# Layer norm stage of an attention and mixture-of-experts kernel written out two tiles ahead, with its row sums on two other engines and the expert padding moved to the setup

## The reference, cut to what matters

```python
x = x + gnn(layernorm(x), adj, W_q, b_q, W_k, b_k, W_v, b_v)
x = x + ffn(layernorm(x), Wr, Wg_s, Wu_s, Wd_s, Wg, Wu, Wd)

# gnn
q = e @ W_q.T + b_q;  k = e @ W_k.T + b_k;  v = e @ W_v.T + b_v
z = (q @ k.T) / sqrt(512) * adj
z = where(z == 0, -10000, z)
out = relu(softmax(z, axis=1) @ v)

# ffn: router softmax over 8 experts, the top 2 of each row with a softmax of their weights
shared = (silu(X @ Wg_s) * (X @ Wu_s)) @ Wd_s
out = shared + sum over the chosen experts of weight * (silu(X @ Wg[e]) * (X @ Wu[e])) @ Wd[e]
```

## Time and profile before

| what | us |
|---|---|
| median of three runs | 1493.55 |
| the profiled execution | 1493.32 |
| its span (first to last instruction) | 1491.6 |
| TensorE busy | 1425.8 (96%) |
| VectorE busy | 681.7 (46%) |
| ScalarE busy | 438.0 (29%) |
| GpSimd busy | 175.4 (12%) |

### The profile page before, as it was taken

One profiled execution on the slowest core, in us unless ns is written; L12 is line 12 of the kernel. 1 busy time (PEld: TensorE's weight loads), 2 busy tenths in 40 slices (PEclk: granted clock), 3 DMA queues, 4 the chain that ended last, 5 costly groups with the idle time before them and its releaser, 6 DMA issues.

```text
span 1491.6 us, 20252 instructions
## 1 busy us (share of the span) xinstructions
PE 1425.8 (96%) x7140; PEld 1227.6 (82%) x7140; DVE 681.7 (46%) x1465; ACT 438.0 (29%) x683; POOL 175.4 (12%) x233
## 2 busy tenths in 40 slices
PE   5889999999999998489999999999999999999998
PEld 3768888888888876369898989889898989888887
DVE  4875566566566565424234332424233435232222
ACT  2331221221221234124334332424233434231111
POOL 1220012112112122001101011010101010100000
PEclk8999999999999999789999999999999999999999
DMA  7311123223223156517252525134252525441000
GB/s 272 123 64 71 57 71 113 70 70 113 70 70 112 67 174 212 56 46 210 50 191 36 191 43 187 35 84 141 43 191 43 184 60 173 111 151 57 0 29 29
DMA packets 85888, 151.75 MB, mean 102 GB/s; under 512 B 14512, under 2 KB 24752, under 8 KB 83504
## 3 DMA queue, kind: packets, MB, share of 16 engines
q1 hardware_dynamic: 68672, 117.79, 24.1%
q0 software_dynamic: 9760, 18.93, 6.5%
q10 hardware_dynamic: 7392, 14.16, 2.8%
HBM read 109.90 MB, written 42.01 MB: 102 GB/s over the span
## 4 chain that ended last, share of the span: by engine, by line
PE 92%; issue 3%; DVE 2%; ACTq 1%; DMA 1%; ACT 0%; POOL 0%; DVEq 0%; SPq 0%; POOLq 0%
PE bank L230 86%; PE bank L649 2%; ACTq L925 1%; PE bank L671 1%; PE bank L802 1%; PE bank L851 1%; DMA owners<-owner,idx 0%; PE bank L665 0%; PE bank L599 0%; PE bank L579 0%; PE bank L809 0%; DMA wq_raw<-in_L_gnn_W_q_dram 0%; PE bank L621 0%; DVE stat L1153 0%; ACT v_h L892 0%
## 5 line engine op out<-in xcount | busy, mean ns | idle before, releaser
L1481 DVE TENSOR_TENSOR hid<-bank,hid 128x384 f32<-128x384 f32 (+1 forms) x96 | 57.8, 602 | 364.6 <-PE bank L230 364.6
L230 PE MATMUL bank<-dn_h,hT_h 128*128 128x512 f32 x416 | 168.3, 405 | 0.9 <-DVE counts L1380 0.6
L230 PE MATMUL bank<-dn_h,hT_l 128*128 128x512 f32 x416 | 163.9, 394 | 0.0
L230 PE MATMUL bank<-dn_l,hT_h 128*128 128x512 f32 x416 | 163.6, 393 | 0.0
L230 PE MATMUL bank<-xq_h,gate_h 128*128 128x384 f32 (+1 forms) x384 | 137.0, 357 | 4.7 <-DVE gate_l L1149 4.4
L230 PE MATMUL bank<-xq_h,gate_l 128*128 128x384 f32 (+1 forms) x384 | 136.6, 356 | 0.0
L230 PE MATMUL bank<-xq_l,gate_h 128*128 128x384 f32 (+1 forms) x384 | 136.5, 355 | 0.0
L230 PE MATMUL bank<-xq_h,up_h 128*128 128x384 f32 (+1 forms) x384 | 135.5, 353 | 0.0
L230 PE MATMUL bank<-xq_h,up_l 128*128 128x384 f32 (+1 forms) x384 | 135.4, 353 | 0.0
L230 PE MATMUL bank<-xq_l,up_h 128*128 128x384 f32 (+1 forms) x384 | 135.3, 352 | 0.0
L1050 ACT ACTIVATE hid<-bank 128x384 f32<-128x384 f32 (+1 forms) x96 | 50.6, 527 | 233.0 <-PE bank L230 232.9
(11 more groups left out here) (213 smaller groups left out, 2751.0 us busy)
## 6 DMA issues: line engine op xcount, KB each, us to landing
adj_t<-in_adj_dram SPq DMA_DIRECT2D x16, 1024.0 KB, 5.8
gate_raw<-in_L_ffn_Wg_dram SPq DMA_DIRECT2D x16, 1024.0 KB, 5.6
up_raw<-in_L_ffn_Wu_dram SPq DMA_DIRECT2D x16, 1024.0 KB, 10.2
dn_raw<-in_L_ffn_Wd_dram SPq DMA_DIRECT2D x16, 1024.0 KB, 12.4
x_t<-in_x_dram SPq DMA_DIRECT2D x32, 256.0 KB, 6.4
slots<-x2row ACTq DMA_DIRECT2D x8, 1024.0 KB, 11.8
e_x<-slots ACTq DMA_DIRECT2D x22, 256.0 KB, 2.7
acc<-x SPq DMA_DIRECT2D x16, 256.0 KB, 2.0
```

What stands on the lines that cost most here:

```text
L230: mm = pe.matmul(o, lhs(a, c), rhs(b, c), start=first and n == 1, stop=last and n == 3 * len(chunks))
L1481: dve.tensor_tensor(hid[:, c % 2, 0:w], bank[2 + c % 2][:, 0:w], hid[:, c % 2, 0:w], ALU.mult).then_inc(sem("hid"), 1)
```

## The change

1. The weights of q and k are loaded, copied and subtracted in four parts each, with a semaphore for each part. The first c2 matmul waits for one part instead of the whole. The first two tiles of x are loaded ahead of W_v.
2. The bias products come directly after c2, in bank 7. The order on TensorE is now: c2, biases, A chunks 0 and 1, turning W_v, A chunk 2, turn tile 0, A chunk 3, turn tile 1.
3. `before_attention` is gone. Each engine runs 16 tiles without a loop, turned and normalised two tiles ahead of the values. ScalarE writes xnT_h directly and VectorE xnT_l directly; xT_h, xT_l and GpSimd's copy are gone. x has four places in place of two.
4. The row sum is made by GpSimd (xn times c2 into "spent") and ScalarE (a copy that sums, directly into s_q).
5. The two halves of the first queries stand ahead of the values of tiles 14 and 15.
6. ScalarE issues the clearing in 12 transfers of 512 KB (32 rows of each of the eight regions, from 32 partitions), one in each of the first 12 tiles, for 384 rows a region instead of 512. `owners` is filled whole in the setup by one transfer of 80 partitions.
7. The rows e_x are loaded as soon as the scatters have landed; the padding comes after, writes `slots` only, and never begins inside the first 384 slots. The table takes two more small VectorE operations.
8. The pieces of block 0 are spread by a plan over all eight chunks.

```diff
         def pieces_in(b, c):
-            if b > FIRST_SHARED or not 2 <= c:
+            if b > FIRST_SHARED:
+                return []
+            if b == 0:
+                plan = [(0, k) for k in range(2, PIECES)] + [(1, k) for k in range(PIECES)] + [(2, k) for k in range(PIECES)]
+                ends = [2, 3, 4, 6, 9, 12, 14, 16]
+                return plan[ends[c - 1] if c > 0 else 0:ends[c]]
+            if c < 2:
                 return []
...
-            sp.dma_start(wq_raw[:], w_q.rearrange("(p c) n -> p c n", c=DC)).then_inc(sem("in_wq"), 16)
-            sp.dma_start(wk_raw[:], w_k.rearrange("(p c) n -> p c n", c=DC)).then_inc(sem("in_wk"), 16)
+            for raw, w, name in ((wq_raw, w_q, "wq"), (wk_raw, w_k, "wk")):
+                for c in range(DC):
+                    sp.dma_start(raw[:, c, :], w.rearrange("(p c) n -> p c n", c=DC)[:, c, :]).then_inc(sem(f"in_{name}{c}"), 16)
+            load_x(0)
+            load_x(1)
...
+            load_rows(0)
+            load_rows(1)
             wait(sp, "table", 1)
             wait(sp, "pad_row", 1)
             with sp.Fori(0, E) as e:
...
                 sp.dma_start(slots[bass.ds(end, P), :], pad_row[:]).then_inc(sem("pad_out"), 16)
-                sp.dma_start(owners[bass.ds(end, PAD * P), :].rearrange("(k p) w -> p k w", p=P), pad_owner[:]
-                             ).then_inc(sem("pad_out"), 16)
-            sp.wait_ge(sem("pad_out"), 32 * E)
-            load_rows(0)
-            load_rows(1)
+            sp.wait_ge(sem("pad_out"), 16 * E)
...
+            def bias_terms(t):
+
+
+                wait(pool, "c2_done", 1)
+                wait(pool, "ln1_done", t + 1)
+                wait(pool, "sq_sum", t)
+                pool.tensor_tensor(spent[:], xn[:, t % 2, :], c2_rep[:], ALU.mult).then_inc(sem("sq_terms"), 1)
+
             power(1, 0)
             power(2, 1)
...
+            for t in range(NT):
+                bias_terms(t)
+                if t + 3 <= NT:
+                    power(t + 3, t % 2)
...
+            def values(t):
+
+                wait(pe, "xnT_l", t + 1)
+                wait(pe, "v_l", t - 1)
...
+            for t in range(NT):
+                if t == NT - 2:
+                    pe.wait_ge(sem("A_done"), DC)
+                    queries(0, 0)
+                if t == NT - 1:
+                    pe.wait_ge(sem("yT_f"), 1)
+                    queries(0, 1)
+                values(t)
+                if t + 2 < NT:
+                    turn_input(t + 2)
...
+            def clear(n):
+
+                act.dma_start(slots.rearrange("(e r) d -> r e d", e=E)[n * CLEAR:(n + 1) * CLEAR, :, :],
+                              zero[0:CLEAR, :].rearrange("p (a d) -> p a d", a=1).broadcast_to([CLEAR, E, D])
+                              ).then_inc(sem("cleared"), 16)
...
+            for t in range(NT):
+                if t < CLEARS:
+                    clear(t)
+                if t >= NT - 2:
+                    queries(t + 2 - NT, t + 2 - NT)
+                values(t)
+                if t + 2 < NT:
+                    inputs(t + 2)
+                    bias_sum(t + 2)
...
+            def layer_norm(t):
                 wait(dve, "xn_turned", t - 1)
-                normalise(xn[:, b, :], x_t[:, b, :], t + 1, b).then_inc(sem("ln1_done"), 1)
+                wait(dve, "sq_terms", t - 1)
+                normalise(xn[:, t % 2, :], x_place(t), t + 1, t % 2).then_inc(sem("ln1_done"), 1)
...
+            for t in range(NT):
+                if t + 2 < NT:
+                    layer_norm(t + 2)
+                if t + 3 < NT:
+                    measure(t + 3)
+                if 0 < t < NT - 1:
+                    inputs(t + 1)
+                if t > 0:
+                    values(t - 1)
```

More of the change, by code:

```diff
@@ L585, in _ @@
                 mm.then_inc(sem("wv_turned"), 1)
[L586 to L610, removed]
             pe.wait_ge(sem("c2_done"), 1)
             A_chunk(2)
+            pe.wait_ge(sem("wvT_l"), 1)
+            turn_input(0)
+            pe.wait_ge(sem("c1_done"), 2)
             A_chunk(3)
[L614 to L628, removed]
+            pe.wait_ge(sem("wvT_l"), DC)
+            turn_input(1)
             def queries(j, half):
@@ L892, in copy @@
                 return act.activation(o, i, ACT.Copy) if scale is None else act.activation(o, i, ACT.Copy, scale=scale)
[L894 to L897, removed]
+            for c in range(DC):
+                act.wait_ge(sem(f"in_wq{c}"), 16)
+                copy(wq["h"][:, c, :], wq_raw[:, c, :]).then_inc(sem("wq_h"), 1)
@@ new lines, in _, with A_chunk @@
+            for c in range(DC):
+                act.wait_ge(sem(f"in_wk{c}"), 16)
+                copy(wk["h"][:, c, :], wk_raw[:, c, :]).then_inc(sem("wk_h"), 1)
+            act.wait_ge(sem("owner_fill"), 2)
+            act.dma_start(owners.rearrange("(p m) w -> p m w", m=2 * P), owner_fill[0:E * REGION // (2 * P), :, :]
+                          ).then_inc(sem("unowned"), 16)
+            def A_chunk(c):
+                wait(act, "A_ps", c + 1)
+                copy(A["h"][:, c, :], bank[4 + c][:]).then_inc(sem("A_h"), 1)
@@ new lines, in inputs, with values, bias_sum @@
+            def inputs(t):
+                wait(act, "xn_turned", t + 1)
+                copy(xnT["h"][:, :, t * P:(t + 1) * P], bank[t % 2][:].rearrange("p (c q) -> p c q", c=DC)).then_inc(sem("xnT_h"), 1)
+            def values(t):
+                wait(act, "v_ps", t + 1)
+                if t == 0:
+                    wait(act, "A_ps", DC)
+                copy(v["h"][:, t, :], bank[2 + t % 2][:]).then_inc(sem("v_h"), 1)
+            def bias_sum(t):
+                wait(act, "sq_terms", t + 1)
+                act.activation(spent[:], spent[:], ACT.Copy, accum_out=s_q[:, t:t + 1]).then_inc(sem("sq_sum"), 1)
@@ L898, in _ @@
+            def clear(n):
+                act.dma_start(slots.rearrange("(e r) d -> r e d", e=E)[n * CLEAR:(n + 1) * CLEAR, :, :],
+                              zero[0:CLEAR, :].rearrange("p (a d) -> p a d", a=1).broadcast_to([CLEAR, E, D])
+                              ).then_inc(sem("cleared"), 16)
+            A_chunk(0)
             for c in range(DC):
                 wait(act, "wv_turned", c + 1)
+                wait(act, "biases", 1)
+                wait(act, "wk_l", DC)
                 copy(wvT["h"][:, c, :], bank[c][:]).then_inc(sem("wvT_h"), 1)
[L902 to L916, removed]
-                    wait(act, "xT1_h", t + 1)
-                    copy(xnT["h"][:, :, bass.ds(t * P, P)], xT1["h"][:, b, :, :].bitcast(F32)).then_inc(sem("xnT_h"), 1)
-                if prev:
-                    wait(act, "v_ps", t)
-                    copy(v["h"][:, bass.ds(t - 1, 1), :], bank[3 - b][:].rearrange("p (a n) -> p a n", a=1)).then_inc(sem("v_h"), 1)
@@ L932, in _ @@
[L932 to L936 removed]
+                if c == 0:
+                    A_chunk(1)
+            A_chunk(2)
+            inputs(0)
+            A_chunk(3)
+            bias_sum(0)
+            inputs(1)
+            bias_sum(1)
+            act.wait_ge(sem("zero"), 1)
@@ L1115, in expert_block @@
                         piece(u, k)
-                    if b == 0 and c == 1:
-                        for k in range(2, PIECES):
-                            piece(0, k)
             def tail_tile(t):
```

243 lines of the change are left out of this document (106 added, 137 removed).

## The result

The changed kernel takes 1439.12 us (median of four runs, 1438.95 to 1439.38) against 1493.38 us before, run beside it. The ratio is 0.9638, with a 95% interval of 0.9621 to 0.9654. The forecast was 1440.3 us. The profiled execution has a span of 1437.6 us, 54.0 less than before.

What follows compares the result with a forecast made beforehand. TensorE bounds the kernel, busy 1425.8 of 1491.6 us, with nearly all idle time in setup with normalisation and expert block 0. Gains of 19.8, 1.7 and 31.5 us give a span of 1438.6, forecast 1440.3 us, range 1431 to 1451.

Steps and rivals of the forecast that it cites:

- bias products end: Setup: 40 bias records directly behind c2 take 4.3 us and end at 15.2 us.
- A chunks 0, 1 end: Setup: these matmuls take 5.5 us plus 1.6 for lower clock behind the biases, ending at 22.3 us.
- filling the pipeline: First normalisation tile: VectorE waits for power and product with nothing else to do, 1.2 us once.
- a tile: Normalisation: VectorE's chain, with xn slowed beside GpSimd's product, sets 3.55 us per tile; TensorE waits 0.3 us in each.
- first scores: End of setup and normalisation: scores start directly at 92.9 us instead of 112.65, a gain of 19.8 us.
- clock in the first scores: First 72 score matmuls: without the gap ahead of them they avoid the lower clock, saving 1.7 us.
- wait at chunk 4, and its clock: Block 0 of the experts: a new 2.8 us wait for VectorE's piece (1, 1), then probably 1.7 us of lower clock.
- The two big terms: Setup: 9.5 us of TensorE idle from ScalarE's clearing go; block 0: the 27.35 us wait behind the padding goes.
- rival 1: Normalisation: TensorE sets the pace, 3.25 us a tile, for a total of 1431.6 us; chance 0.12.
- Rival 2: Normalisation: clears from 32 partitions at half pace hold ScalarE, 4.45 us a tile, total 1451 us; chance 0.09.
- Rival 3: Normalisation: clears hold ScalarE longer; 6.2 us each uses up the gain, 7 us gives 1503 us; chance 0.02.
- Rival 4: Block 0: the row wait returns as a wait for scatters landing after over 20 us, 1454 us; chance 0.03.

Runs made afterwards that it cites:

- e1: Changed kernel, but the two loads of expert 0's rows stand behind the padding and its wait again; 1455.57 us, 16.5 more.
- e2: Changed kernel, but all 12 clearing transfers are issued in one row ahead of tile 0 instead of one per tile; 1460.45 us, 21.3 more.
- e4: Changed kernel, but GpSimd's product and the row sum cover only 128 of the 512 columns (row sums wrong); 1439.59 us.
- e5: Changed kernel, but block 0 has its pieces where they were before: four in chunk 1, then two per chunk; 1440.61 us, 1.5 more.
- e9: Changed kernel, but all clears are issued ahead of tile 0, from 128 partitions in eight transfers of 768 KB; 1449.76 us, 10.6 more.
- e7: Changed kernel, but the bias products stand behind A chunks 0 and 1 instead of ahead of them; 1438.66 us, 0.5 less.

## Why the prediction was right, step by step

| step | forecast | measured |
|---|---|---|
| c2 starts | 5.2 us | 5.58 |
| c2 ends | 10.9 | 12.0 |
| bias products end | 15.2 | 17.9 |
| A chunks 0, 1 end | 22.3 | 25.2 |
| filling the pipeline | 1.2 | 1.6 |
| a tile | 3.55 | 3.21 |
| product on GpSimd | 1.2 | 1.28 |
| first scores | 92.9 | 91.1 |
| clock in the first scores | -1.7 | -1.7 |
| VectorE's list in chunk 3 | 8.27 | 8.24 |
| wait at chunk 4, and its clock | 2.8, 1.7 | 3.0, 1.83 |
| wait for the rows | none | none |

**The two big terms** stood as forecast: no clearing on the chain and no wait for the padding. e1 and e2 show how much each order is worth in the changed kernel, 16.5 and 21.3 us. Neither is the size of the term: 16.2 us of waiting come back of the 27.35, and the clears from 32 partitions would cost more than the 9.5 us that they cost before.

**Two terms of the sum were mis-sized, and cancelled in part.** The setup came out 2.9 us too cheap in my sum at the end of A chunk 1. I had priced the bias products at the full clock and charged the lower clock once, to the matmuls behind them. In this run the block begins at full clock, falls to the lower one within itself (5.91 us instead of 4.28) and still leaves it to the A chunks (7.27 instead of 5.50, near what I charged). c2 started 0.4 us later than forecast and was 0.7 us longer than before, too; the cause of that is open. The sizes differ between programs with the same setup, as told above, but A chunk 1 ends later than 22.3 us in all their traces (23.97 in e1 is the earliest). The tile pace was 0.34 us too dear. Its chain is right piece by piece, but the measurement takes 1.0 us without the loop's register operations (51.61 to 52.62), the power 0.52 and xn's end comes 0.28 us behind the product instead of 0.45: 3.17, which falls just under TensorE's 3.21. So rival 1's pace came true, by a margin of 0.04 us, and e4 confirms that TensorE is the bound. 14 x 0.34 = 4.8 us back, against 2.9 and the longer filling. That the total came within 1.2 us of the forecast is owed in part to this cancelling, and so to luck: the pace of the tile was forecast for the wrong bound, VectorE's chain with TensorE waiting 0.3 us in each tile, where TensorE in fact has no wait once the pipeline is filled.

**Block 0.** The 36 matmuls up to the second turned rows end at 598.77, against 652.22 before: 53.45 us earlier. The first stages won 23.2 us (21.5 and 1.7 of clock), of which 0.2 were lost again in attention: the eight router matmuls in block 0 (L671 before, L687 now) start at 546.76 against 569.74, 22.98 us earlier. So block 0 gave 30.5 us where the sum has 31.5. Of the 1.0, 0.3 are in the wait of chunk 4 and its clock, 0.5 in the 36 matmuls themselves (8.72 instead of 8.24), and 0.3 in the two short routing matmuls, which now wait ahead of chunk 2's up (from 553.15 to 553.56, against 0.12 us before). The remaining 0.5 us of the 54.0 lie behind these rows; I can't place them.

**The rivals.** Rival 2, clears that hold ScalarE, did not happen in the changed kernel, whose issues stay at 0.32 to 0.34 us, but the half pace that it assumed is there: e2 has 2.27 us for each issue and 209 GB/s. It is hidden because a tile takes 3.21 us, so the queue drains faster than it fills (512 KB at 209 GB/s are 2.5 us, an estimate from e2). Rival 3 would have needed 6.2 us for each. Rival 4 was far off, the scatters had landed by 568.06. That the plan of pieces is nearly worth nothing (6.25 us won, 4.7 lost) stood in the forecast's sum, and e5 measures 1.5 us with 0.6 of it in the setup.

## What to carry to other kernels

A transfer's issue is free only while its queue has room; spread long transfers over a stage in which the engine that issues them has slack, and check that each is moved in less time than one step takes (here some 2.5 us against 3.21). Ask of every wait at the end of a preparation (padding, tables) whether what follows really reads it: here a reordering of two loads was worth 16 us. And where an engine makes operands in between other small work, order its list by who waits soonest: moving one subtraction ahead of 21 small operations gave 4.7 us. Before a difference of one or two microseconds is put down to an edit, compare the stages that the edit does not touch: here the setup alone differed by 3.6 us between programs with the same code.

## What the runs showed of the hardware that I had not expected

- Zeros sent from 32 partitions moved at 209 GB/s (e2, 46 to 50 us), and from 128 at 409 (e9, the same window), with the DMA engines shown busy in both (0.97 and 1.05). The busy share did not tell the two apart.
- A block of 40 short matmul records ran from full to half clock within itself: 5.91 us in the changed kernel instead of 4.28 to 4.5, with a granted clock of 0.50 from 15 us on. TensorE operations behind it paid as well, whichever they were (7.27 us for 24 matmuls, or 3.28 for 16 transposes in e7). In other programs with the same setup the block took 4.60 to 6.74 us.
- Two issues of 768 KB (e9) or of 512 KB (e2) passed without holding ScalarE. From there each issue lasted 2.0 to 2.4 us in e2 and 0.9 to 1.8 in e9, somewhat less than its transfer takes at the rates above (2.5 and 1.9 us, estimates from them).
